# Masked cross-attention: the mask enters the scores through TensorE instead of VectorE

## The reference, cut to what matters

```
q, k, v = heads(x @ wq + bq), heads(ctx @ wk + bk), heads(ctx @ wv + bv)   # 16 heads of 8, 128 queries, 77 keys
logits  = einsum('bhqd,bhkd->bhqk', q, k) / sqrt(8)
logits  = logits + (1.0 - mask) * -1e9                                     # the same mask for all 16 heads
attn    = softmax(logits) * group_prob                                     # the gate, the same for all heads
out     = (attn @ v) merged @ wo + bo
```

## Time and profile before

| what | value |
|---|---|
| time, median of 3 runs | 5596.02 us (5586.29 to 5598.56) |
| the profiled execution: time / span | 5577.15 us / 5575.1 us |
| granted TensorE clock, mean of the span | 0.855 of 2.4 GHz |
| busy share of the span: TensorE / VectorE / ScalarE / GpSimd | 72% / 81% / 50% / 56% |
| the masked stage x0 | 2655 to 3260 us, 605 us, 256 steps of 2.36 us |

### The profile page before, as it was taken

One profiled execution on the slowest core, in us unless ns is written; L12 is line 12 of the kernel. 1 busy time (PEld: TensorE's weight loads), 2 busy tenths in 40 slices (PEclk: granted clock), 3 DMA queues, 4 the chain that ended last, 5 costly groups with the idle time before them and its releaser, 6 DMA issues. The chain is left out here.

```text
span 5575.1 us, 103824 instructions
## 1 busy us (share of the span) xinstructions
PE 4029.1 (72%) x29177; PEld 2314.7 (42%) x29180; DVE 4512.3 (81%) x8773; ACT 2779.2 (50%) x6405; POOL 3140.3 (56%) x3422
## 2 busy tenths in 40 slices
PE   5777778777777787774777748887283888689943
PEld 2333233332333333332455536666283666456621
DVE  5999999999999999996898877776246777667778
ACT  3545555455555554552677734445374455345434
POOL 6877777777777777775565643324544222233302
PEclk8999989988998999987888869997696888799965
DMA  2111111011101110111545526666115555366511
GB/s 82 65 52 48 67 67 67 36 65 67 66 33 67 67 67 36 65 65 28 100 87 86 94 55 107 112 110 166 48 60 118 96 101 95 67 114 119 104 40 30
DMA packets 320172, 420.38 MB, mean 75 GB/s; under 512 B 40000, under 2 KB 301712, under 8 KB 309136
## 3 DMA queue, kind: packets, MB, share of 16 engines
q1 hardware_dynamic: 315536, 408.35, 31.4%
q0 software_dynamic: 4352, 8.95, 0.5%
HBM read 307.65 MB, written 109.58 MB: 75 GB/s over the span
## 5 line engine op out<-in xcount | busy, mean ns | idle before, releaser
L2184 POOL TENSOR_TENSOR m_h<-m_dtu,m_Bb 128x512 f32<-128x512 f32 x1024 | 1589.5, 1582 | 229.3 <-PE bank L1819 223.1
L1819 PE MATMUL bank<-m_h,ident 128*128 128x512 f32 x2048 | 1211.3, 682 | 500.1 <-DVE m_h L2083 487.2
L1819 PEld LDWEIGHTS bank<-m_h,ident 128*128 128x128 f32 x2048 | 362.0, 206 | 1163.3 <-DVE m_h L2083 1014.9
L2077 DVE TENSOR_TENSOR_SCAN m_h<-m_dA,m_h 128x512 f32<-128x512 f32 x512 | 750.5, 1466 | 6.3 <-DVE m_sz L2010 6.3
L2083 DVE TENSOR_TENSOR m_h<-m_h,bank 128x512 f32<-128x512 f32 x1024 | 674.2, 659 | 5.2 <-issue 3.4
L2077 DVE TENSOR_TENSOR_SCAN m_h<-bank,m_h 128x512 f32<-128x512 f32 x512 | 621.3, 1214 | 27.9 <-DVE m_sz L2010 11.9
L1966 ACT ACTIVATE bank<-m_dt,m_A 128x512 f32<-128x512 f32 x512 | 352.3, 688 | 495.6 <-DVE m_h L2077 435.5
L1966 ACT ACTIVATE m_dA<-m_dt,m_A 128x512 f32<-128x512 f32 x512 | 367.2, 717 | 429.4 <-DVE m_h L2077 425.6
L516 ACT ACTIVATE x_sm<-x_sm,x_nm 128x77 f32<-128x77 f32 x1024 | 353.5, 349 | 113.3 <-DVE x_nm L679 112.9
L861 POOL TENSOR_TENSOR x_sm<-x_sm,x_gp 128x308 f32<-128x308 f32 x256 | 219.5, 860 | 132.3 <-ACT x_sm L516 132.3
L377 PE MATMUL bank<-ident,x_sm 128*77 128x128 f32 x1024 | 195.9, 322 | 134.5 <-DVE x_pT L702 121.5
(11 more groups left out here) (422 smaller groups left out, 10560.0 us busy)
## 6 DMA issues: line engine op xcount, KB each, us to landing
m_Bb<-m_B SPq DMA_DIRECT2D x32, 4096.0 KB, 12.0
x_Ks<-x_k_parts SPq DMA_DIRECT2D x32, 462.0 KB
x_q_parts<-x_qp SPq DMA_DIRECT2D x32, 384.0 KB, 4.0
x_Qs<-x_q_parts SPq DMA_DIRECT2D x32, 384.0 KB
f_Ks<-f_k_parts SPq DMA_DIRECT2D x16, 768.0 KB
a_Ks<-a_k_parts SPq DMA_DIRECT2D x16, 768.0 KB
x_xp<-x_stage SPq DMA_DIRECT2D x32, 256.0 KB
x_Qs<-x_q_parts SPq DMA_DIRECT2D x32, 256.0 KB
```

Source lines behind the costliest of these rows:

```text
L1819: pe.matmul(banks[4 + c], ident[:], h[:, k % RING, :], start=(s == 0), stop=(s == NS - 1)).then_inc(s_ya.sem, 1)
L2077: v.tensor_tensor_scan(h[:, k % RING, :], decays[k % AHEAD], h[:, k % RING, :], 0.0, ALU.mult, ALU.add).then_inc(s_h.sem, 1)
L2184: pool.tensor_tensor(h[:, k % RING, :], dtu[:, d, c, :], Bb[:, d, s, :], ALU.mult).then_inc(s_dB.sem, 1)
```

## The change

The mask is now added on TensorE. A constant pair of diagonal 128 x 128 bf16 matrices, `hide`, holds -61 * 2^17 and -9 * 2^9; the tile `hidden` (bf16, was x_neg in f32) holds 0 where the mask is 1 and 125 where it is 0. The two products `hide[part]` times `hidden` (broadcast over four heads, 308 columns) open the accumulation in the bank and sum to exactly -1e9 at the hidden places; the four score products then add to it. VectorE's addition L676 is gone, and its maximum reads the bank. ScalarE's exponential reads the bank too and writes x_sm, so the bank is held until the exponential is done: the scores of step k wait for the exponential of step k - 2 (`s_read`), where they waited for the addition of step k - 2. The wait for x_sm to be free (transposes of two sequences before) moves from VectorE to ScalarE. GpSimd fills `hide` by two memsets and two diagonal selects before `s_setup`.

```diff
+MASK = (125.0, 61.0 * 2 ** 17, 9.0 * 2 ** 9)
...
-        neg = sb("neg", [P, 2, GB, S2]) if mask is not None else None
+        hidden = sb("hidden", [P, 2, GB, S2], BF16) if mask is not None else None
+        hide = sb("hide", [P, 2, P], BF16) if mask is not None else None
...
+        s_read = s_Sf if gate is None else s_e
...  (scores)
+                    if mask is not None:
+                        pe.wait_ge(s_neg.sem, s_neg.at(2 * i + l + 1))
-                pe.wait_ge(s_Sf.sem, s_Sf.at(b, c + 1 - 2))
+                pe.wait_ge(s_read.sem, s_read.at(b, c + 1 - 2))
+                if mask is not None:
+                    o = bankS[c % 2][:, 0:4 * sk].rearrange("p (h k) -> p h k", h=4)
+                    for part in range(2):
+                        pe.matmul(o, hide[:, part, :], hidden[:, l, q, :].unsqueeze(1).to_broadcast([P, 4, S2]),
+                                  start=(part == 0), stop=False)
                 for h in range(4):
                     hh = 4 * c + h
                     ins = pe.matmul(bankS[c % 2][:, h * sk:(h + 1) * sk], Qs[:, l, hh, q * S:(q + 1) * S],
-                                    Ks[:, l, hh, q * sk:(q + 1) * sk], start=True, stop=True)
+                                    Ks[:, l, hh, q * sk:(q + 1) * sk], start=(mask is None), stop=(mask is None or h == 3))
...  (exp_rows)
                 act.wait_ge(s_mx.sem, s_mx.at(b, c + 1))
+                if c == 0:
+                    act.wait_ge(s_tw.sem, s_tw.at(b - 1))
-                    ins = act.activation(sm[:, lm % 2, h, :], sm[:, lm % 2, h, :], ACT.Exp, bias=nm[:, lm % 2, 0, h:h + 1],
+                    ins = act.activation(sm[:, lm % 2, h, :], bankS[c % 2][:, (h - 4 * c) * S2:(h - 4 * c + 1) * S2], ACT.Exp, bias=nm[:, lm % 2, 0, h:h + 1],
...  (masks)
-                v.wait_ge(s_Sf.sem, s_Sf.at((g - 1) * GB))
-                v.tensor_scalar(neg[:, par], mi[:], 1.0, 1e9, ALU.subtract, ALU.mult).then_inc(s_neg.sem, 1)
+                v.wait_ge(s_S.sem, s_S.at((g - 1) * GB))
+                v.tensor_scalar(hidden[:, par], mi[:], 1.0, -MASK[0], ALU.subtract, ALU.mult).then_inc(s_neg.sem, 1)
...  (maximum)
-                if mask is not None:
-                    hs = slice(4 * c, 4 * c + 4)
-                    if c == 0:
-                        v.wait_ge(s_tw.sem, s_tw.at(b - 1))
-                    v.tensor_tensor(sm[:, p, hs, :], src, neg[:, l, q, :].unsqueeze(1).to_broadcast([P, 4, S2]),
-                                    ALU.add).then_inc(s_Sf.sem, 1)
-                    v.wait_ge(s_Sf.sem, s_Sf.at(b, c + 1))
-                    v.tensor_reduce(nm[:, p, 0, hs], sm[:, p, hs, :], AX.X, ALU.max, negate=True).then_inc(s_mx.sem, 1)
-                else:
-                    v.tensor_reduce(nm[:, p, 0, 4 * c:4 * c + 4], src, AX.X, ALU.max, negate=True).then_inc(s_Sf.sem, 1)
+                ready = s_Sf if mask is None else s_mx
+                v.tensor_reduce(nm[:, p, 0, 4 * c:4 * c + 4], src, AX.X, ALU.max, negate=True).then_inc(ready.sem, 1)
...  (gpsimd, before s_setup)
+            if mask is not None:
+                for part in range(2):
+                    pool.wait_ge(s_pool, n)
+                    pool.memset(hide[:, part, :], 0.0).then_inc(s_pool, 1)
+                    pool.wait_ge(s_pool, n + 1)
+                    pool.affine_select(out=hide[:, part, :], in_=hide[:, part, :], compare_op=ALU.not_equal, fill=-MASK[1 + part], base=0,
+                                       pattern=[[-1, P]], channel_multiplier=1).then_inc(s_pool, 1)
+                    n += 2
```

More of the change, by code:

```diff
@@ L453, in _ @@
             pe.wait_ge(s_zero.sem, NZ)
+            if mask is not None:
+                pe.wait_ge(s_setup.sem, 1)
             turn(0, first=True)
@@ L514, in exp_rows @@
                 act.sem_inc(s_step, 1)
+                if c == 0:
+                    act.wait_ge(s_tw.sem, s_tw.at(b - 1))
+                    act.sem_inc(s_step, 1)
                 for h in range(4 * c, 4 * c + 4):
-                    ins = act.activation(sm[:, lm % 2, h, :], sm[:, lm % 2, h, :], ACT.Exp, bias=nm[:, lm % 2, 0, h:h + 1],
+                    ins = act.activation(sm[:, lm % 2, h, :], bankS[c % 2][:, (h - 4 * c) * S2:(h - 4 * c + 1) * S2], ACT.Exp, bias=nm[:, lm % 2, 0, h:h + 1],
                                          accum_out=den[:, lm, h:h + 1])
```

## The result

| | before | after |
|---|---|---|
| time, median | 5591.66 us (4 runs, 5586.29 to 5598.56) | 5527.39 us (4 runs, 5516.31 to 5546.52) |
| profiled execution: time / span | 5577.15 / 5575.1 us | 5516.31 / 5514.6 us |
| granted TensorE clock, mean | 0.855 | 0.866 |

The account below looks back on a forecast made before the run. VectorE was taken to bound x0; after the change TensorE's 385 + 66 = 451 us at 82% gives 550 us instead of 605, a gain of 55 less 1.3 for setup: 5596 - 54 = 5542 us, range 5484 to 5600.

Parts of the forecast that it names:

- The bound: In x0 VectorE leads, busy 539.7 of 605 us; without the addition's 120.7 us it needs 419 us.
- how densely TensorE can be used: x0 after: TensorE's 451 us of full-clock work at an 82% share makes the stage 550 us.
- the first rival: In x0 the four engines mesh as in x1, at 91%: stage 495 us, total 5487 us; chance 0.19.
- My cross-check: In a 550 us x0, VectorE's 419 us are 76%, which is what f0, a1 and x1 show.
- -25 and 0: Ends in us for ScalarE's change in x0 from reading exponentials out of PSUM; counted as nothing.
- The new wait: Scores waiting for the exponential two steps before: a loop of 2.65 us per two steps, forecast to take 4.3.
- the second rival: x0's loop through the bank decides, with other work ahead: stage 576 us, total 5568 us; chance 0.16.
- The fourth rival: Mask products' broadcast operand read at f32 price: TensorE work 559 us, x0 614 us, slower by 10; chance 0.02.
- The third rival: TensorE at a low clock becomes x0's bound after new idle gaps: stage 614 us, total 5606 us; chance 0.09.
- Setup: Two memsets and two selects on GpSimd at x0's start add 1.3 us, at least 0, at most 2.
- The other stages should keep their lengths within 3 us each.: Sign: all stages other than x0 stay within 3 us of their lengths before.

Follow-up runs that it names:

- before_products: Kernel before plus two unused 308-column TensorE products ahead of each step's scores, which overwrite them, and 128 idle instructions: 5567.79 us, ratio 0.9982.
- addition_back: Changed kernel with 125 idle instructions, plus an unused VectorE addition of zeros ahead of each maximum: 5560.17 us, ratio 0.9963.

## Why the prediction was right, and where it was not

**The bound.** Right. x0 was bound by VectorE, and putting 120.7 us of addition back costs 72 us. (the earlier trace rows leave out the largest single wait in x0, GpSimd's 132.3 us for the exponential; VectorE's two rows together are still more.) Its need after, 422 us, and TensorE's, 451 us at full clock, were forecast within 1%.

**"The stage's length is then set by how densely TensorE can be used ... 82%."** This step failed. The runs with none and one product show that TensorE's load doesn't set the length until the second product; and where it does, at four, TensorE reaches 95%, far above the 82% that I took. So the share in f0 and a1 was no ceiling of the code. That it showed those stages' waits for others is my reading; no run tested those stages. The loop took 513 us in place of 550. It lies 29 above the 484 that the prediction gave for VectorE with its old idle time, and 18 above the first rival's 495. That rival was the nearest for x0: the clock went to 0.99, as in x1, where I had forecast 0.92 to 0.95. My cross-check, "VectorE is then at 76%", was no check, since it took its share from the same three stages; VectorE is at 421.74 / 513 = 82%.

**What I had no term for: the clock gives time back.** In the forecast the clock only turned busy time into work. before_products shows 16 us of x0 that come with the higher clock, with VectorE as loaded as before. In the changed kernel the clock rises without the products too (0.98 with none), so either the products or the missing addition is enough to raise it. The split of the 92.7 us into 72 and 21 therefore holds for taking the addition back alone; taken apart in another order the parts would differ.

**ScalarE.** Counted at nothing, with "-25 and 0" as ends. The exponential's duration fell from 349 to 335 ns, inside the forecast, but its accumulator read rose from 189 to 217. ScalarE's busy time in the loop is 386.52 us, 15 below the 401 that I gave as its lower end. What counts is start to start, and that fell from 0.34 us to 0.30. Before, then after:

```profile
3011.69 0.34 ACT L516 ACTIVATE x_sm<-x_sm,x_nm 128x77 f32<-128x77 f32 x1
...
3012.03 0.34 ACT L516 ACTIVATE x_sm<-x_sm,x_nm 128x77 f32<-128x77 f32 x1
```

```profile
3001.74 0.33 ACT L531 ACTIVATE x_sm<-bank,x_nm 128x77 f32<-128x77 f32 x1
3001.94 0.21 ACT L531 ACTIVATION_READ_ACCUMULATOR x_sm<-bank,x_nm 128x1 f32 x1
3002.04 0.34 ACT L531 ACTIVATE x_sm<-bank,x_nm 128x77 f32<-128x77 f32 x1
3002.24 0.22 ACT L531 ACTIVATION_READ_ACCUMULATOR x_sm<-bank,x_nm 128x1 f32 x1
3002.34 0.34 ACT L531 ACTIVATE x_sm<-bank,x_nm 128x77 f32<-128x77 f32 x1
```

That is 0.16 us less from the maximum to the gate in each step. It is one candidate for the 5 us of x0 that neither the addition nor the clock explains (21 - 16); I did not test it alone. Another is GpSimd's gate, whose mean in the windows of 2700 to 3120 us is 837 ns in addition_back and 868 before. The Trainium skill's "VectorE: DVE Perf Modes", section "The TRN2 errata — SBUF-src ops pay a fixed extra latency per instruction", gives ScalarE a smaller fixed cost out of PSUM than out of SBUF (172 against 224 cycles at 1.2 GHz, 43 ns); the spacing's 40 ns agrees, the durations' 14 doesn't.

**The new wait** was priced rightly: nearly free alone (2 us), 59.6 us of it in the changed kernel, and the second rival's loop through the bank did not close.

**The mask products** cost what bf16 products of their size should. The fourth rival priced itself too low, since it took TensorE at 91% where the sum took 82%; at 82% its 559 us of work would have been a stage of 682 us. It is out all the same: 298 ns, and from the start of two of them to the scores behind them it is 0.27 us, with 0.26 forecast:

```profile
3000.69 0.44 PE L355 MATMUL bank<-x_hidden,x_hide 128*128 128x308 bf16 x2
3000.96 0.30 PE L359 MATMUL bank<-x_Ks,x_Qs 128*128 128x77 bf16 x4
```

**The third rival**, a low clock, was the opposite of what happened: the gaps of 2 us were waits for VectorE's copies, and they went with the addition.

**Setup.** x_Qs is zeroed from 2619.78 us, 2.58 behind the start of x_vB's memset; before, x_Qs followed at 2618.17, 1.13 behind, so 1.45 us more, with 1.3 forecast:

```profile
2617.20 0.95 POOL L800 MEMSET x_vB<- 128x1024 f32 x1 [13.33 <-DMA x_bob<-in_L_xattn_wo_b]
...
2619.78 13.75 POOL L824 MEMSET x_Qs<- 128x16384 bf16 x1 [0.15 <-POOL x_hide L819]
```

**"The other stages should keep their lengths within 3 us each."** This failed too. x1 lost 13 to 17 us, since TensorE's longer code in x0 shifted the loops behind it. The ratio of 0.9842 with the code shifted back against 0.9902 as written puts the whole loss at 0.6%, 34 us, or some 20 to 47 with both intervals; the two profiled spans differ by 26, of which x1 has 17.

So the total of 5542 came near 5527 because two errors of opposite sign met, and that is luck: 39 us too little gain in x0, and behind it, in the profiled execution, 17 us of loss in x1, which the code's place explains, and 17 in f0 and what follows, which the kernel before shows by itself in some executions. I had no term for either. By its parts the prediction was right on direction, bound and needs, and wrong on what stands behind the bound.

**The better version.** The changed kernel with 125 idle instructions ahead of x0's work computes the same and takes 5491.86 us, 1.6% below before instead of 1.0%. With one mask product (and 61 of them) it is 5481.0 us, 1.8% below, where -999,424,000 will do for -1e9; that differs from the reference only in rows that are hidden altogether.

## What to carry to other kernels

When the leading engine loses work, don't set the next bound by the share that an engine reaches in stages where it waits for others; work out each engine's need, take the leader's old idle time as the first guess, and treat the other's share as a ceiling only where something shows it full. Here work added to a TensorE with gaps raised its granted clock, and was free or better than free as long as VectorE led and the clock was still low; at a clock of 1.00 the second product of a step already cost 9 us. And when an unrolled list changes its length, compare the stages behind it: a few hundred instructions moved a later loop by 2 to 3%, and 125 idle ones brought it back.

## What the runs showed of the hardware that I had not expected

- TensorE's code position is worth some 34 us by the ratios in either kernel (1.0061 with 131 idle instructions, 0.9842 against 0.9902 with 125), of which 17 and 23 us are seen in x1, with stops of 2.7 to 4.5 us there that the profile puts down to no engine.
- Useless products raised the granted clock from 0.84 to 0.95 and shortened the stage by 16 us (646.4 against 662.3).
- A bf16 product whose operand is one 77-column row block repeated four times costs as much as one that reads 308 columns plainly would by the other rows' slope (298 ns).
- VectorE's conversion of 128 x 308 from int32 to bf16 took 1400 ns where it began 0.05 us behind GpSimd's addition (1.27 us), and 310 ns, bf16 or f32, where it began 0.3 to 0.4 us behind; then the addition took 1.76 to 1.82 us.
- An exponential with an accumulated sum is issued every 0.30 us out of PSUM and every 0.34 out of SBUF, though its two recorded parts sum to 552 ns in the first case and 538 in the second.
